# One attention and FFN layer on one core: block 0 by eight plain products, pair 0's order, and the loads of bias and Wo

## The reference

```python
x = x + xattn(layernorm(x), ctx)      # q = ln(x) @ Wq, k = ctx @ Wk, v = ctx @ Wv   (1024 x 512) @ (512 x 4096)
                                      # score = q k^T / sqrt(128) + position_bias[b, h, 64, 64], masked softmax
                                      # (probs @ v) @ Wo                             (1024 x 4096) @ (4096 x 512)
x = x + ffn(layernorm(x))             # x @ base_W^T + base_b + sum over experts of LoRA, weighted by the router
```

## Time and profile before

| | |
|---|---|
| median of 3 runs | 836.3 us (834.69 to 837.33) |
| profiled execution: its own time / span in the trace | 835.49 us / 833.7 us |
| outside the span (time minus span) | 1.79 us |
| mean granted clock of TensorE | 0.983 of full speed |

### The profile page before, as it was taken

How to read it: one execution, slowest core, us unless ns; L and a number is a source line. 1 busy time by engine, 2 the same in 40 slices (tenths; PEclk the granted TensorE clock), 3 DMA queues, 4 the chain that set the end, 5 groups by cost and what they waited for, 6 DMA issues and landing times.

```text
span 833.7 us, 16300 instructions
## 1 busy us (share of the span) xinstructions
PE 803.3 (96%) x6352; PEld 652.7 (78%) x6352; DVE 579.5 (70%) x1020; ACT 340.5 (41%) x655; POOL 244.6 (29%) x232
## 2 busy tenths in 40 slices
PE   6799999999999999879999999999999999998998
PEld 4588888888888888657888887888887878886786
DVE  5674435157677665479887888788888888858872
ACT  4453525245555555243334433344334433333410
POOL 3340422114334332253233322333133322111340
PEclk9799999999999999889999999999999999999999
DMA  5436674234545554565554445453553435442002
GB/s 201 153 112 205 213 240 145 110 127 153 173 156 157 184 163 118 203 183 160 175 162 121 118 133 178 118 159 100 158 173 111 138 112 153 114 148 47 1 8 94
DMA packets 108074, 118.35 MB, mean 142 GB/s; under 512 B 44239, under 2 KB 77007, under 8 KB 107998
## 3 DMA queue, kind: packets, MB, share of 16 engines
q1 hardware_dynamic: 107998, 117.31, 44.9%
HBM read 81.64 MB, written 35.65 MB: 141 GB/s over the span
## 4 chain that ended last, share of the span: by engine, by line
PE 88%; DVE 4%; DMA 3%; issue 2%; POOL 2%; SPq 1%; ACT 1%; POOLq 0%; DVEq 0%; ACTq 0%
PE pP L1177 38%; PE pY L1177 37%; PE pO L1309 4%; PE pS L1284 4%; PE pO L1177 2%; PE pT_ L1294 2%; DMA wk_raw<-in_L_xattn_Wq 1%; DMA wv_raw<-in_L_xattn_Wv 1%; SPq L391 1%; POOL wv_lo L537 1%; POOL twv L550 0%; PE pT_ L1211 0%; PE pS L1211 0%; PE pO L1211 0%; DVE y L990 0%
## 5 line engine op out<-in xcount | busy, mean ns | idle before, releaser
L990 DVE TENSOR_TENSOR y<-y,pY 128x512 f32<-128x512 f32 x124 | 84.4, 681 | 40.6 <-PE pY L1177 40.2
L1177 PE MATMUL pP<-xo_hi,wk_hi 128*128 128x512 f32 x224 | 98.4, 439 | 3.4 <-DVE q L817 3.4
L1177 PE MATMUL pY<-wo_hi,oT_hi 128*128 128x512 f32 x248 | 97.9, 395 | 2.4 <-DVE y L990 2.4
L1177 PE MATMUL pY<-wo_lo,oT_hi 128*128 128x512 f32 x248 | 96.9, 391 | 0.0
L1177 PE MATMUL pY<-wo_hi,oT_lo 128*128 128x512 f32 x248 | 96.6, 390 | 0.0
L807 DVE TENSOR_TENSOR wk_lo<-twk,wk_hi 128x256 fp32r<-128x256 f32 x128 | 79.4, 631 | 24.5 <-ACT wk_hi L631 24.5
L1177 PE MATMUL pP<-xo_lo,wk_hi 128*128 128x512 f32 x224 | 89.7, 400 | 0.0
L1177 PE MATMUL pP<-xo_hi,wk_lo 128*128 128x512 f32 x224 | 89.4, 399 | 0.0
L533 POOL TENSOR_TENSOR bias<-bias,madd 128x512 f32<-128x512 f32 x32 | 42.1, 1316 | 140.4 <-DMA bias<-in_fside_Bx32xSxS 140.4
L631 ACT CAST wk_hi<-twk 128x256 fp32r<-128x256 f32 x128 | 52.1, 408 | 57.1 <-PE pP L1177 45.7
L807 DVE TENSOR_TENSOR wk_lo<-wk_raw,wk_hi 128x256 fp32r<-128x256 f32 x96 | 50.9, 530 | 24.8 <-ACT wk_hi L631 24.8
(11 more groups left out here) (235 smaller groups left out, 1889.8 us busy)
## 6 DMA issues: line engine op xcount, KB each, us to landing
v_hbm<-stage SPq DMA_DIRECT2D x64, 256.0 KB, 2.2
k_hbm<-stage SPq DMA_DIRECT2D x64, 256.0 KB, 3.6
k<-k_hbm SPq DMA_DIRECT2D x16, 1024.0 KB, 5.5
v<-v_hbm SPq DMA_DIRECT2D x16, 1024.0 KB, 6.2
wk_raw<-in_L_xattn_Wk SPq DMA_DIRECT2D x16, 512.0 KB, 4.4
wk_raw<-in_L_xattn_Wq SPq DMA_DIRECT2D x16, 512.0 KB, 4.4
bias<-in_fside_Bx32xSxS SPq DMA_DIRECT2D x128, 64.0 KB, 2.8
wo_raw<-in_L_xattn_Wo SPq DMA_DIRECT2D x16, 512.0 KB, 3.7
```

Source lines behind the costliest of these rows:

```text
L990: nc.vector.tensor_tensor(y[:, t, :], y[:, t, :], src[:, :], ALU.add).then_inc(y_added, 1)
L1177: mm = nc.tensor.matmul(bank_, a, b, start=first and n == 0, stop=last and n == len(terms) - 1, skip_group_check=read_between)
```

## The change

1. **Block 0 by eight plain products.** C11 = A11 B11 + A12 B21, C21 = A21 B11 + A22 B21, C12 = A11 B12 + A12 B22, C22 = A21 B12 + A22 B22, each summed in PSUM, in four pairs of products. Two small tiles `a21` and `b12` are split for this. ACT copies the four results out (`piece_of_first`). The A sums of tile pair 0, which block 4 needs, are made in step 2, after transposing tiles 0 and 4 again (eight transposes more). The A sums are made in the order 1, 2, 3, 0.
2. **Weight sums of set 0 are all DVE's**, and so are all its `lower_w`; POOL does nothing in them. `load_ctx(5)` goes ahead of the last quarter of Wv.
3. **Pair 0** runs scores(0), (33,1), (33,2), scores(1), (33,6), (33,7), turn_p(0), (33,5), times_v(0), turn_p(1), (33,3), times_v(1), (33,4); ACT's order follows, and DVE makes c11 of block 33 ahead of weights(0).
4. **Loads.** Bias of head 0 goes to the end of SP's step 28, of head 1 to step 29, Wo's first part to step 20.

```diff
-ORDER = [(0, 1), (1, 1), (0, 2), (1, 2), (0, 6), (0, 7), (0, 5), (0, 3), (0, 4), (1, 6), (1, 7), (1, 5)]
+ORDER = [(1, 1), (0, 2), (1, 2), (0, 4), (0, 3), (0, 7), (1, 6), (1, 7), (1, 5), (2, 1), (1, 3), (2, 2), (1, 4),
+         (2, 6), (2, 7), (2, 5)]
...
+            load_ctx(5)
             load_wv0(1, 1)
-            load_ctx(5)
...
-                if n == 30:
+                if n == 20:
+                    load_wo(0)
+                if n in (28, 29):
                     sp.wait_ge(as_lo, 8)
-                    load_bias(0)
-                    load_bias(1)
-                    load_wo(0)
+                    load_bias(n - 28)
...
@@ ACT, start @@
+            last_high(0)
+            act.wait_ge(turned, SECOND_TURN[0] + 1)
+            nc.scalar.copy(a21[0][:, :, :], second_turn(0)[:, 0:2 * P].rearrange("p (c t) -> p c t", c=2)
+                           ).then_inc(a21_h, 1)
+            wait_raw(act, 0, (0, 1))
+            nc.scalar.copy(b12[0][:, :, :], raw_block(0, 0, 1)).then_inc(b12_h, 1)
+            rows_out(1)
+            last_high(1)
+            higher(0, 5)
+            piece_of_first(0, 2, pP[0], c11_made)
+            copy_p1(1)
+            sums_high(1)
             higher(0, 3)
             higher(0, 2)
+            piece_of_first(2, 4, pP[1], c21_made)
+            piece_of_first(1, 3, pP[0], c12_made)
+            piece_of_first(3, 7, pP[1], c22_made)
             higher(0, 4)
...
@@ ACT, steps 1 and 2: after sums_high(j) @@
+                if n == 1:
+                    higher(0, 6)
+                if n == 2:
+                    rows_out(0)
                 copy_v(n)
+                if n == 2:
+                    sums_high(0)
...
@@ DVE, start, after lower_w(0, 0), first_low(0), first_low(1), lower_w(0, 1) @@
+            dve.wait_ge(a21_h, 1)
+            last_low(0)
+            lower(a21[1][:, :, :], second_turn(0)[:, 0:2 * P].rearrange("p (c t) -> p c t", c=2), a21[0][:, :, :],
+                  a21_l)
+            dve.wait_ge(b12_h, 1)
+            lower(b12[1][:, :, :], raw_block(0, 0, 1), b12[0][:, :, :], b12_l)
+            lower_w(0, 5)
+            first_t3()
+            first_t2()
+            sums_of_a(1)
+            sums_low(1)
             lower_w(0, 2)
+            make_c11(1)
+            lower_w(0, 3)
+            first_t1()
             lower_w(0, 4)
+            first_t4()
...
@@ PE, start, after C11 and (1, 2) @@
+            pe.wait_ge(a21_l, 1)
+            product(pP[1][:, :], a21_b11, last=False)
+            pe.wait_ge(a6_lo, 1)
+            product(pP[1][:, :], a22_b21, first=False).then_inc(prod, 1)
+            pe.wait_ge(c11_made, 1)
+            pe.wait_ge(b12_l, 1)
+            product(pP[0][:, :], a11_b12, last=False)
+            pe.wait_ge(w_lo[5], 1)
+            product(pP[0][:, :], a12_b22, first=False).then_inc(prod, 1)
+            pe.wait_ge(c21_made, 1)
+            product(pP[1][:, :], a21_b12, last=False)
+            product(pP[1][:, :], a22_b22, first=False).then_inc(prod, 1)
             turn_pair(2)
...
+                if n == 2:
+                    pe.wait_ge(a6_lo, 3)
+                    turn(ctx[:, 0, :], first_turn(0))
+                    turn(ctx[:, 4, :], second_turn(0))
...
@@ PE, pair 0 @@
+                if i == 0:
+                    scores(0)
+                    times(n, 1)
+                    times(n, 2)
+                    scores(1)
+                    times(n, 6)
+                    times(n, 7)
+                    turn_p(0)
+                    times(n, 5)
+                    times_v(0)
+                    turn_p(1)
+                    times(n, 3)
+                    times_v(1)
+                    times(n, 4)
+                    continue
...
@@ ACT, pair 0 @@
+                if i == 0:
+                    higher(w, 0)
+                    exp(0)
+                    higher(w, 1)
+                    copy_u(n)
+                    higher(w, 2)
+                    higher(w, 3)
+                    turned_p(0)
+                    exp(1)
+                    copy_v(n)
...
@@ DVE, pair 0 @@
+                if i == 0:
+                    make_c11(n)
                 weights(h)
                 add_tile(i - 1, 0)
                 scores(h + 1)
-                make_c11(n)
+                if i > 0:
+                    make_c11(n)
```

More of the change, by code:

```diff
@@ L624, in higher @@
                     act.wait_ge(prod, DONE[last_of(w - 1), PROD[slot]])
-                if w == 0 and slot == 4:
-                    act.wait_ge(t1_first, 1)
-                elif slot in TW:
+                if slot in TW:
                     act.wait_ge(tw_made, 4 * w + 1 + TW[slot])
@@ L637, in first_high, with rows_out, last_high @@
                                first_turn(j)[:, :].rearrange("p (k c t) -> p k c t", k=2, c=2)).then_inc(a01_hi, 1)
-            def second_rows(j):
+            def rows_out(j):
+                act.wait_ge(turned, AGAIN[1] + 1 if j == 0 else SECOND_TURN[j] + 1)
+                if j != 1:
+                    act.wait_ge(sum_step, 4 * SUM_ORDER.index(j))
+                nc.scalar.copy(low[j // 4][:, :, :], second_turn(j)[:, :].rearrange("p (c t) -> p c t", c=DC)
+                               ).then_inc(low_made, 1)
+            def last_high(j):
                 cols = tile_cols(j)
                 act.wait_ge(turned, SECOND_TURN[j] + 1)
[L643 to L646, removed]
                 nc.scalar.copy(a_part(j, 0)[:, 6, :, cols],
@@ L696, in _ @@
                     first_high(j)
-                    second_rows(j)
+                    rows_out(j)
+                    last_high(j)
                 copy_u(n)
@@ L959, in _ @@
                     sums_low(j)
+                if n == 1:
+                    lower_w(0, 6)
+                if n == 2:
+                    sums_of_a(0)
                 make_c22(n)
+                if n == 2:
+                    sums_low(0)
                 if w is not None:
@@ L1179, in product, with of_slots @@
                 return mm
+            def of_slots(j, slot, w):
+                cols, hi, lo = tile_cols(j), w_part(w, 0), w_part(w, 1)
+                return [((co_hi[:, slot, c, cols], co_lo[:, slot, c, cols]), (hi[:, slot, c, :], lo[:, slot, c, :]))
+                        for c in range(2)]
             def times(n, p):
@@ L1184, in times @@
                 pe.wait_ge(w_lo[slot], w + 1)
-                if n < 4 or n == QA:
-                    j = n if n < 4 else 7
-                    pe.wait_ge(a01_lo if slot < 2 else (a6_lo if slot == 6 else as_lo), j + 1)
+                if n <= 4 or n == QA:
+                    j = 7 if n == QA else n % 4
+                    if 2 <= slot <= 5:
+                        pe.wait_ge(as_lo, SUM_ORDER.index(j) + 1)
+                    else:
+                        pe.wait_ge(a6_lo if slot == 6 else a01_lo, j + 1)
                 if p in (1, 2):
                     before = n - 1 if n > QA else n - 2
-                    if before >= 0:
+                    if n == 2:
+                        pe.wait_ge(c12_made if p == 1 else c22_made, 1)
+                    elif before >= 0:
                         pe.wait_ge(c12_made if p == 1 else c21_made, before + 1)
                 else:
-                    pe.wait_ge({6: c1_made, 7: c11_made, 5: u_made, 3: v_made, 4: c22_made}[p], n + 1)
+                    pe.wait_ge({6: c1_made, 7: c11_made, 5: u_made, 3: v_made, 4: c22_made}[p],
+                               n + 1 if p in (7, 4) else n)
                 hi, lo = w_part(w, 0), w_part(w, 1)
                 if n < NV:
-                    cols = tile_cols(n)
-                    pairs = [((co_hi[:, slot, c, cols], co_lo[:, slot, c, cols]), (hi[:, slot, c, :], lo[:, slot, c, :]))
-                             for c in range(2)]
+                    pairs = of_slots(n, slot, w)
                 else:
@@ L1235, in _ @@
             pe.wait_ge(made, 1)
+            cols0 = tile_cols(0)
+            a21_b12 = [((a21[0][:, c, :], a21[1][:, c, :]), (b12[0][:, c, :], b12[1][:, c, :])) for c in range(2)]
+            a11_b12 = [((co_hi[:, 0, c, cols0], co_lo[:, 0, c, cols0]), (b12[0][:, c, :], b12[1][:, c, :]))
+                       for c in range(2)]
+            a21_b11 = [((a21[0][:, c, :], a21[1][:, c, :]), (wv_hi[:, 0, c, :], wv_lo[:, 0, c, :])) for c in range(2)]
+            a22_b21 = [((co_hi[:, 6, c, cols0], co_lo[:, 6, c, cols0]), (wv_hi[:, 1, c, :], wv_lo[:, 1, c, :]))
+                       for c in range(2)]
+            a12_b22 = [((co_hi[:, 1, c, cols0], co_lo[:, 1, c, cols0]), (wv_hi[:, 5, c, :], wv_lo[:, 5, c, :]))
+                       for c in range(2)]
+            a22_b22 = [((co_hi[:, 6, c, cols0], co_lo[:, 6, c, cols0]), (wv_hi[:, 5, c, :], wv_lo[:, 5, c, :]))
+                       for c in range(2)]
             warm_up(8)
```

152 lines of the change are left out of this document (83 added, 69 removed).

## The result

| | before | changed |
|---|---|---|
| median | 836.2 us (8 runs) | 832.5 us (8 runs, 830.51 to 836.52) |
| ratio, 95% interval | | 0.995, 0.9931 to 0.997 |
| span of the profiled execution | 833.7 us | 830.7 us |

The change makes the kernel faster, by 0.5% (4.2 us by the ratio, 2.5 to 5.8 by its interval). 9 us were forecast.

The account below looks back on a forecast made before the run. PE, busy 96% of the span, was taken as the bound, so only its stops or lower clock could be won. Start 1.2, block 2 -0.2, loads and pair 0 8.0 gave 9.0 us: 827 us, range 822.5 to 832.

Parts of the forecast that it names:

- The walk through the start up to (2,6): Block 0 to block 2: PE stops of 5.2 and 2.1 us, (2,6) starting at 45.6 us against 48.2 before.
- c22 of block 2 ... a slowing of 1.9 leaves 0.5 us at most. I cost it at 0.2: Block 2: DVE's sums beside POOL's delay c22, which (2,4) waits for; cost 0.2 us, up to 2 in the range.
- the sign that the prediction had named as proof against it: Blocks 2 to 31: any PE stop appearing there would show the prediction wrong.
- Is wanted at 55.9: Block 2: (2,4) wants c22 at 55.9 us, and c22 would be ready at 54.5.
- The start's term, +1.2: Start up to (2,6): 1.2 us won, between 3.8 won without a clock fall and 1.5 lost.
- The loads' term, 6.4: Block 32: moved loads win 6.4 us, 3.4 of the stop, 2.7 of the clock, 0.3 of small gaps.
- Pair 0's term, 2.0: Pair 0: the new order wins 2.0 us after the loads' 6.4, up to the second half of scores(2).
- POOL's add_mask at 0.4: Pair 0: POOL's add_mask beside weights(1) may take 0.4 us of the gain.
- B: Start: gives nothing, both new stops with the lower clock use up the gain; 828.3 to 829.8 us, chance 0.22.
- C: Pair 0 gives nothing or weights land late again: middle gives 5.5, start 1; 829.8 to 832 us, chance 0.12.
- E: Start: five DVE instructions at the pace beside POOL cost 9.7 us; 836.7, or 839 from 4 us each; chance 0.06.

Follow-up runs that it names:

- the start alone: The changed kernel with the loads and pair 0 put back as before, leaving only the new start; ratio 1.002 to the kernel before.
- C21 early: The changed kernel with ACT's copy of C21 ahead of sums_high(1), higher(0,3) and higher(0,2); ratio 0.9946 to the kernel before.
- the second trace of before: The kernel before, unchanged, profiled once more; 319.6 us from tile 5's transposes to block 32, 39.8 us from there to scores(2).
- the loads alone: The kernel before with only SP's moved loads (bias to steps 28 and 29, Wo to step 20); ratio 0.9937 to the kernel before.
- the third kernel with the edit: The kernel before with moved loads, pair 0's order and Wo's split early, start as before; ratio 0.9944 to the kernel before.
- the two other moves: Wo's split of pair 0 early and ACT's copy of C21 early, added to the changed kernel with tile pair 0 early; ratio 0.9857 to the kernel before.
- Wo early: The changed kernel with Wo's cast and lowering for pair 0 put where ACT and POOL wait for set 22; ratio 0.9939 to the kernel before.
- POOL waits: The changed kernel with POOL's sums of weight set 1 waiting until c22 of block 2 is made; ratio 0.9979 to the kernel before.
- loads and pair 0: The kernel before with the moved loads and pair 0's new order, the start as before; ratio 0.9946 to the kernel before.

## Why the prediction was wrong

The direction was right, the size was not: 9.3 us foreseen on the scale of the medians, 4.2 measured.

- **What held.** The walk through the start up to (2,6): stops of 5.0 and 1.9 us for 5.2 and 2.1, (2,6) at 46.4 for 45.6 (the clock did fall after both stops). load_wv(1) at 34.4 and POOL's sums at 44.1, as foreseen. Block 32 without a stop, done at 347.1, 12.8 us after its start (12.6 in the forecast).
- **The step that failed first is "c22 of block 2 ... a slowing of 1.9 leaves 0.5 us at most. I cost it at 0.2".** I let one of DVE's instructions collide with POOL. Two stand in a row, sums_low(3) and the first of tile 0's sums, and each has to wait for the end of one of POOL's: 1.8 and 2.0 us longer. The stop is 2.2 us, and the clock fell after it, which costs (2,4) another 1.5: 3.7 us instead of 0.2. (Of five traces with this stop the clock fell in three; it stayed up in the start alone and in C21 early.) That POOL is what slows them is shown: making POOL wait brings the two instructions to 1.23 and 0.43 and takes the stop away. It was also the sign that the prediction had named as proof against it, a stop in blocks 2 to 31. The prediction had the rule of the Trainium skill beside it (page "SBUF — State Buffer", section "Who interferes with whom"), that each pair of such instructions excludes each other for the whole instruction. It named sums_low(3), the first of tile 0's sums and sums_low(0). The trace agrees for the first two, 2.99 and 2.44 us, each ending just after one of POOL's; sums_low(0) came when POOL was done and took 1.23. I took a single row's 1.94 for the sum instead of one for each.
- **The slack in that step was wrong too.** "Is wanted at 55.9" does not follow from (2,6) at 45.6: six products lie between, which take 8.4 us in the changed kernel, so (2,4) was wanted at 54.0 and c22 at 54.5 would have been late without any collision. In fact c22 without a collision is ready near 53 us (52.6 with POOL waiting) and was wanted at 54.8: 1.8 us of slack, enough for one collision and not for two. The two errors of time hid each other; the number of collisions did not.
- **The start's term, +1.2, was also taken from a quick start.** From tile 5's transposes to block 32 the profile of before took 317.6 us; four other traces of the old start have 319.5, 319.6, 320.2 and 320.5. Against these the new start with its collision (319.1 to 320.1) is worth nothing either way, and the 2.4 us by which block 32 starts later in the changed kernel's profile are mostly this. What it wins up to (2,6), 3.2 us against the second trace of before (32.1 and 35.3 after tile 5's transposes), the 3.7 us of the step above take back.
- **The loads' term, 6.4, is nearly right for an execution in which the clock falls** (6.0 between the marks). 2.7 of it are the lower clock after the stop in block 32. It fell in one of three traces. Without the fall the stage takes 39.8 us, and the loads give 2.6. Over many runs the ratio gives 5.3 (3.3 to 7.3), which doesn't tell the two apart.
- **Pair 0's term, 2.0, measured 0.2** beside the loads alone. The place where it is lost is the end of DVE's list: weights lowered beside POOL's add_mask and wo_lo, then `oT_lo`, c22 and c21. I had costed POOL's add_mask at 0.4 and had not asked what wo_lo, which now comes earlier, stands beside. With Wo's split moved, that lowering falls from 1.99 to 0.63 us and the middle is 34.8 and 34.5, against 35.2 to 37.0 in the five traces without the edit whose set 22 landed as promptly. So the collision is shown; how much of the 2 us it accounts for, from 0.4 to all, the traces leave open. In the third kernel with the edit the late landing of set 22 covers it.
- **The whole, by the ratios.** The loads alone give 5.3 us, with pair 0 it is 4.5, with the start 4.2; foreseen were 6.4, 8.0 and 9.0. So of the 4.8 us that are missing some 2.4 belong to pair 0, 1.3 to the start and 1.1 to the loads. Each single difference is uncertain by 2 to 3 us; the total, 2.5 to 5.8, is clear of the 9.0.
- **Rivals.** The outcome is nearest to B and C together: the start gives nothing, pair 0 nothing, the loads all or half. I had each with its own chance and none for both. E's mechanism (DVE beside POOL) was the right one, in another place: I had looked for it in the first 40 us, where POOL is idle. (E's 839 us for 4 us each is also a wrong sum: five times 2.77 on 827 is 841. Nothing hangs on it.)

What stays open: what decides whether the clock falls after a stop of 2 to 3 us, why set 22 lands 1.4 us later relative to its issue in some executions, and what the executions of the start alone that took 838 to 843 us did.

## What to carry to other kernels

When work is moved in time, list what each engine does beside it in the new place, not only whether the result is early enough: here three instructions of 0.4 to 1.2 us became 2 to 3 us because another engine's block of work stood beside them, and moving one group of instructions some 13 us earlier, into an idle stretch, turned a change worth 4 us into one worth 7 (12 with the two other moves). Price a stop without the clock's fall and with it, and take neither as certain from one profile. Before a term is read as a difference to one execution's timeline, see how much that stretch differs between executions; distances between marks inside one trace are sharper than its absolute times.

## What the runs showed of the hardware

The granted clock fell from 2.4 to 1.2 GHz after some stops of PE of 1.8 to 3.4 us and not after others, and after the very same stop in one execution and not in the next. Block 32: with the 3.4 us of the first profile, not after 2.9 us in two others. Block 2, 2.2 us: in the changed kernel, its second trace and Wo early, not in the start alone and C21 early. Before the second half of scores(2), 1.9 us: in the changed kernel, not in POOL waits and C21 early. In pair 0 of loads and pair 0, not after 2.8 us. Before (33,7): after 1.8 us in C21 early, not after 1.7 us in the changed kernel. What a fall cost: six matmuls took 2.88 us instead of 1.36, twelve 5.46 instead of 3.0.

The first loads let PE wait 0.2 us for tile 1 in one execution of the changed kernel and 1.5 in the other; set 22 took 6.48 us to land in the one and 7.90 in the other.

A DVE instruction with two SBUF inputs beside one of POOL's took 2.99 us for 1.23, 2.44 for 0.42 and 1.99 for 0.42; in the first case POOL's next one took 3.38 for 2.39. DVE's instructions with one input in PSUM kept their 0.42 and 0.68 beside POOL.
